# Attention loop: the outputs' turn moved from a head group's first step into its third

## The reference

```python
qkv = einsum('bsd,df->bsf', x, Wqkv) + bqkv        # 32 query heads, 8 key and value heads of 8
k = repeat(k, 4, axis=2); v = repeat(v, 4, axis=2)
scores = einsum('bqhd,bkhd->bhqk', q, k) / sqrt(8)
attn = softmax(scores, axis=-1)
out = einsum('bhqk,bkhd->bqhd', attn, v).reshape(b, s, 256)
return einsum('bsd,de->bse', out, Wo) + bo
```

## Time and profile before

| what | us |
|---|---|
| median of 3 runs | 661.53 (659.85 to 665.92) |
| profiled execution, own time | 660.77 |
| its span in the trace | 659.0 |
| TensorE busy in the span | 614.3 (93%) |
| VectorE busy | 395.3 (60%) |
| ScalarE busy | 327.2 (50%) |
| GpSimd busy | 251.4 (38%) |
| maxima, 256 of 682 ns | 156.6 busy |
| exponentials, 256 of 603 ns | 136.5 busy |

### The profile page before, as it was taken

One profiled execution on the slowest core, in us unless ns is written; L12 is line 12 of the kernel. 1 busy time (PEld: TensorE's weight loads), 2 busy tenths in 40 slices (PEclk: granted clock), 3 DMA queues, 4 the chain that ended last, 5 costly groups with the idle time before them and its releaser, 6 DMA issues.

```text
span 659.0 us, 11841 instructions
## 1 busy us (share of the span) xinstructions
PE 614.3 (93%) x4298; PEld 405.0 (61%) x4298; DVE 395.3 (60%) x916; ACT 327.2 (50%) x654; POOL 251.4 (38%) x331
## 2 busy tenths in 40 slices
PE   3999999999999989999979999999999999999990
PEld 2887887888788775566666444444444445556650
DVE  5426705732670578433366989898989955743326
ACT  4523423432342234244315589898989875423322
POOL 5870561282065063413333033635253520431331
PEclk9999999999999999999979999999999999999995
DMA  6101200300189993222389994000000000031213
GB/s 223 33 1 33 97 0 6 124 1 1 33 262 298 109 261 124 87 67 81 108 254 346 304 178 4 1 2 1 2 2 1 1 2 1 17 98 53 85 57 127
DMA packets 69000, 57.40 MB, mean 87 GB/s; under 512 B 21520, under 2 KB 64400, under 8 KB 68944
## 3 DMA queue, kind: packets, MB, share of 16 engines
q1 hardware_dynamic: 66736, 50.60, 31.6%
q0 software_dynamic: 2208, 6.05, 2.5%
HBM read 30.78 MB, written 25.85 MB: 86 GB/s over the span
## 4 chain that ended last, share of the span: by engine, by line
PE 79%; DVE 9%; DMA 4%; ACT 3%; POOL 2%; issue 2%; another core or an unknown queue 1%; SPq 0%; ACTq 0%; POOLq 0%; DVEq 0%
PE psum L1670 10%; PE psum L306 9%; PE psum L308 9%; PE psum L307 9%; PE psum L1303 8%; PE psum L1642 8%; PE psum L1630 5%; PE psum L1332 4%; PE psum L1655 4%; DVE stat L655 2%; PE psum L1227 2%; PE psum L1600 2%; DVE mx L1782 1%; PE psum L1213 1%; PE psum L1220 1%
## 5 line engine op out<-in xcount | busy, mean ns | idle before, releaser
L1782 DVE TENSOR_REDUCE mx<-psum 128x1 f32<-128x512 f32 x256 | 156.6, 682 | 17.9 <-PE psum L1642 17.9
L1528 ACT ACTIVATE pr<-psum 128x512 f32<-128x512 f32 x256 | 136.5, 603 | 25.6 <-PE psum L1655 25.5
L1655 PE MATMUL psum<-qT,kT 32*128 32x512 f32 x256 | 77.5, 494 | 1.1 <-ACT pr L1528 1.1
L1670 PE MATMUL psum<-pr,vals 128*32 128x256 f32 x1024 | 77.6, 389 | 0.0
L1642 PE MATMUL psum<-kT,qT 32*128 32x512 f32 x256 | 64.4, 493 | 0.9 <-ACT qT L1495 0.7
L613 POOL DMA_INDIRECT routed_y<-yr,xg x30 | 28.7, 957 | 83.0 <-DVE yr L865 82.4
L1303 PE MATMUL psum<-w_gu,xgT 128*128 x120 | 56.4, 592 | 0.0
L1642 PEld LDWEIGHTS psum<-kT,qT 32*128 32x128 f32 x256 | 24.2, 181 | 43.7 <-DVE mx L1782 21.8
L856 DVE SCALAR_TENSOR_TENSOR h<-psum,xg,sg 128x256 f32<-128x256 f32 x30 | 14.5, 484 | 49.8 <-ACT sg L1058 49.8
L576 POOL TENSOR_TENSOR ksum_t<-k_hi 128x1024 f32<-128x1024 f32 x8 | 19.2, 2401 | 64.6 <-DVE k_lo L803 64.4
L1580 POOL CAST mp<-mx 128x16 bf16<-128x16 f32 x16 | 3.1, 197 | 105.8 <-DVE mx L1782 105.8
(11 more groups left out here) (218 smaller groups left out, 1419.0 us busy)
## 6 DMA issues: line engine op xcount, KB each, us to landing
sorted_x<-zeros SPq DMA_DIRECT2D x2, 9088.0 KB, 39.9
w_gu<-in_L_ffn_gate_w SPq DMA_DIRECT2D x16, 256.0 KB, 6.7
w_gu<-in_L_ffn_up_w SPq DMA_DIRECT2D x16, 256.0 KB, 6.5
w_d<-in_L_ffn_down_w SPq DMA_DIRECT2D x16, 256.0 KB, 6.4
xg<-sorted_x SPq DMA_DIRECT2D x30, 129.0 KB, 2.1
wk_f<-in_L_attn_Wk SPq DMA_DIRECT2D x4, 512.0 KB, 5.2
wq_f<-in_L_attn_Wq SPq DMA_DIRECT2D x4, 512.0 KB, 5.9
wv_f<-in_L_attn_Wv SPq DMA_DIRECT2D x4, 512.0 KB, 4.0
```

Of the source, the lines that this page charges most:

```text
L1528: nc.scalar.activation(pr[d % 3][:, j], s2_bank(d, j), ACT.Exp, scale=SCALE).then_inc(exp_ready, 1)
L1655: mm(s2_bank(d, j), kT[n // GH][rows, kc * P:(kc + 1) * P], qT2[n % 2][rows, :], start=True, stop=True).then_inc(s2_made, 1)
L1670: last = mm(ps[AV_BANK][j * VW:(j + 1) * VW, cols], vals[:, n // NKV * TB + kc, n % NKV // GH * GH + j, :], pr[d % 3][:, j, cols], start=( ...
L1782: v.tensor_reduce(mx[n % 2][:, t, j:j + 1], s1_bank(c, j), AX.X, ALU.max, negate=True).then_inc(max_read, 1)
```

## The change

The outputs' turn of group n leaves step 4n + 12 (a first step) for step 4n + 14 (a third step). On TensorE it stands ahead of the second half of the first scores instead of behind it. On VectorE its copy stands between the second and the third maximum of the step instead of behind all four. Outputs 13 to 15, in steps 64, 68 and 72, stay where they were. ScalarE's code is unchanged.

```diff
             if c % TB == 0:
-                what = [("q1", c // TB + 1), ("o", (c - 12) // TB)]
+                what = [("q1", c // TB + 1)] + ([("o", (c - 12) // TB)] if c >= STEPS else [])
...
             else:
-                what = []
+                what = [("o", (c - 14) // TB)] if c < STEPS else []
...
             if c_ < STEPS:
-                FOR_DVE += [("s1", c_ * GH + j) for j in range(GH)]
+                FOR_DVE += [("s1", c_ * GH + j) for j in range(2)]
                 FOR_DVE += [x_ for x_ in new if x_[0] == "o"]
+                FOR_DVE += [("s1", c_ * GH + j) for j in range(2, GH)]
...
                 for what in turns_at(c):
-                    if what[0] != "o":
+                    if what[0] != "o" or c < STEPS:
                         turn(what)
                 if c < STEPS:
                     scores1(c, 1)
                 for what in turns_at(c):
-                    if what[0] == "o":
+                    if what[0] == "o" and c >= STEPS:
                         if what[1] == NG - 1:
                             keep_warm(2, SPARE)
                         turn(what)
...
             for c in range(END):
-                n = (c - 12) // TB if c % TB == 0 and c >= 12 else -1
+                now = [n for kind, n in turns_at(c) if kind == "o"]
                 if c < STEPS:
-                    for j in range(GH):
-                        maximum(c, j)
+                    maximum(c, 0)
+                    maximum(c, 1)
+                    for n in now:
+                        outputs(n)
+                    maximum(c, 2)
+                    maximum(c, 3)
                 if QKV_AT <= c < QKV_AT + TB:
                     take(TB + c - QKV_AT)
-                if 0 <= n < NG:
-                    outputs(n)
+                if c >= STEPS:
+                    for n in now:
+                        outputs(n)
```

## The result

The changed kernel is slower by 0.75%: a ratio of 1.0075 to the kernel before, 95% interval 1.0057 to 1.0092, which on 660.3 us is 5.0 us. Its median is 665.75 us against 660.3 for 20 executions of each. The forecast was 666.5 from 661.53, +5.0, with a range of 663.2 to 669.6. Two of the 20 executions of the changed kernel took 1694 and 3168 us and are left out of the ratio (without them the median is 665.63).

The account below looks back on a forecast made before the run. The prediction took the loop to be a ring of TensorE, VectorE and ScalarE; third steps +4.4, first steps -0.1, +1.0 and -0.4, tail +0.2, fourth steps -0.1 gave +5.0, so 666.5 us, range 663.2 to 669.6.

Parts of the forecast that it names:

- ring of three banks: First step: the last second score waits for the second exponential to free a ScalarE bank; 3.37 us instead of 3.50.
- Rival A: First step not held by ScalarE: one slot of 0.43 us less per group, 5.6 us faster, 655.9 us; chance 0.07.
- The third step: Where the outputs' turn goes: 2.63 us, +0.34 rather than the turn's 0.59; 4.4 us over 13 groups.
- the old wait: Third step, second half: the last second score waits for an exponential to free a bank; takes in 0.25 of the turn.
- The carry: ScalarE's lateness from the third step passes through the fourth; ScalarE starts the first step 0.22 to 0.25 us later.
- the alternative 0.53: Second score to exponential takes 0.53 us, not 0.60: carry about 0.1, sum 3.5 to 4.0, 665.3 us.
- Rival B: No carry, ScalarE makes up 0.2 us in the fourth step: 663.9 us; chance 0.10.
- Rival C: VectorE's ring binds and holds the third step's fourth first score for 0.23 us: 3.0 more, 669.5 us; chance 0.11.
- The last touched group: Its first step, without q1: end set by ScalarE instead of VectorE, 3.08 us instead of 3.47, -0.4.
- the earliest first step: The one touched first step without lateness carried in from a group before: -0.1 us.
- the 11 with carry: First steps that ScalarE starts late: 3.59 us instead of 3.50, 11 x 0.09 = 1.0 us.
- tail of +0.2: Behind the last touched group: the tail starts with ScalarE late, +0.2 us.

Follow-up runs that it names:

- e1: Against the kernel before: outputs' turn stays in the first step but stands between the step's halves on TensorE and VectorE; ratio 0.9977.
- e2: Against the kernel before: the 13 outputs' turns left out, VectorE copies a constant from SBUF instead; ratio 0.9968.
- e3: The changed kernel with ScalarE's copy to oT moved behind the exponentials of heads 2 and 3 in touched first steps; ratio to the kernel before 1.0039.
- e6: The changed kernel with one PSUM bank moved from VectorE's ring (three left) to ScalarE's (four); ratio to the kernel before 1.0071.
- e5: The changed kernel with the outputs' turn in the third step but behind the second half of the first scores; ratio to the kernel before 1.0168.
- e4: The changed kernel with only VectorE's copy put back behind the four maxima of the third step; ratio to the kernel before 1.0229.
- e7: On top of e1: second scores issued ahead of first scores in each step's first half, from the 7th step on; ratio to the kernel before 0.9968.

## Why the prediction was right

- **No slot is won in the first step.** Forecast: 3.37 without carry, held by the ring of three banks, although TensorE alone would need 2.49. e1 and e2 gave 3.37 each, e3 and e6 moved only what ScalarE does or owns and shortened the step. Rival A is excluded, and with it the rule that pairing by itself is a gain: it was, by 0.13.
- **The third step pays 0.34 of the turn's 0.59.** Measured 2.64 against 2.30. The rest lies in the old wait; e5 shows that this holds behind the first scores too, where a slot is paid on top.
- **The carry.** Forecast 0.22 to 0.25 from the third exponential of the third step, over the bank wait of the fourth, into ScalarE's start of the first. Measured: exponential 0.59 behind its score (0.60 taken; the alternative 0.53 is out), bank wait 0.22, oT copy at 0.49 instead of 0.28, first step 3.55 to 3.59. e4 removes the carry and finds 3.37. Rival B is excluded.
- **VectorE hides its copy.** No first score of the changed kernel waits for it. Rival C did not happen; e4 shows how near it was: two maxima later, and the copy adds 1.05 to the fourth step, 0.87 to the group.
- **The last touched group.** Its first step was 3.06 after 3.48, -0.4 as said, and for the reason given: it starts at 525.00, and its last second score is released by ScalarE 1.64 into it (1.65 forecast).

```profile
526.64 0.49 PE L1656 MATMUL psum<-qT,kT 32*128 32x512 f32 x1 [0.20 <-ACT pr L1529]
```

- **The sum.** +5.0 forecast, +5.0 by the ratio (3.8 to 6.1). Term by term, in the profiled loop: third steps +4.4 (4.4 forecast), the earliest first step -0.1 (-0.1), the 11 with carry +0.7 (1.0, so this term was 0.3 too large), the last -0.4 (-0.4), fourth steps 0.0 (-0.1): +4.6 against 4.8. The tail of +0.2 cannot be read from the changed kernel's trace, since a dip of the clock lies in it; in e3, which has the same tail and no dip there, it was 0.17 longer than before. That the total came out at 5.0 to the digit is luck. It could not have told the forecast from my alternative of 3.5 to 4.0; the 0.59 of the exponential does. And 666.5 was too high by 0.75, less than the 1.2 by which the median of three that it started from lay above that of 20.

The two parts of the change have opposite signs: "between the halves" alone gained 0.12 per group in the first step, "into the third step" alone lost 0.77, and together they lose 0.4. They do not simply add up: the place between the halves is worth 0.12 per group in the old step and 0.37 in the new one (11.66 to 11.29), because there no bank of ScalarE's holds up the slot it saves.

## What to carry to other kernels

In a ring of engines, an operation that looks like load on the busiest engine may stand in a hole that another engine's bank order has made; before moving it, ask when the next item behind it could start without it. Where it goes to, count how much of it falls into a wait already there, and then follow the delay once around the ring, past the steps whose length does not change: here most of e7's gain in three steps (0.16 of 0.2) was lost in the first step, and in the change a delay made in the third step cost 0.2 in the first, more than the 0.13 won there by taking the turn out, while the step between them kept its length. An engine at 100% busy proved nothing; step lengths over repeated groups resolved hundredths of a microsecond where the total time could hardly tell 0.3%.

## What the runs showed that I had not expected

In the profiled executions of e4, e5, e6 and e7 TensorE's granted clock fell for a short stretch early in the loop, near 380 us, where the other five, the kernel before and the changed kernel among them, kept it. In e5 (columns as in the earlier trace rows):

```profile
376.00:378.50 2.50, 1.95 (x13) 0.97 (x12) 2.40 (x5) 1.91 (x4) 0.00 (x0) 1.00 1.10 329
378.50:382.30 3.80, 3.80 (x29) 1.57 (x28) 3.02 (x5) 2.82 (x6) 2.84 (x10) 0.55 1.12 275
382.30:386.00 3.70, 3.70 (x44) 1.67 (x40) 2.88 (x5) 2.87 (x6) 0.17 (x1) 1.00 1.12 282
```

The step there took 4.89 us against 3.72 in the changed kernel: 1.2 us for one dip to the lower of the two levels (1.2 of 2.4 GHz), ahead of which TensorE had been idle for 0.55 of 2.5 us. That idle time is not what sets these kernels apart: the kernel before was idle for 0.53 of 2.7 us at the same place (376.0 to 378.7 us) and kept 1.00. In e4 and e5 the code up to that step is the same as in kernels that had no dip there, so it is not an effect of their edits that the traces could show.

The changed kernel had its dip elsewhere, behind the loop. The kernel before (first row) had one low stretch in mid-kernel, ahead of the loop, twice as long as the changed kernel's (second row), and none behind it:

```profile
334.30:341.10 6.80, 5.45 (x25) 5.45 (x26) 5.86 (x21) 0.00 (x0) 1.29 (x2) 0.50 0.95 288
...
333.70:337.10 3.40, 2.88 (x13) 2.88 (x14) 3.29 (x14) 0.00 (x0) 0.00 (x0) 0.50 0.98 294
538.50:541.90 3.40, 3.40 (x24) 1.22 (x21) 0.42 (x1) 0.95 (x3) 3.13 (x2) 0.50 0.02 5
```

Ahead of the loop the low stretch was 6.8 us long in the traces of before, e1, e2, e3 and e6, and 3.4 us in those of the changed kernel, e4, e5 and e7; each of the latter had a second one of 3.4 us later, and so had e6. What decides is open; one profiled execution of each kernel can't tell whether it goes with the kernel. For a comparison of two traces it means: take step lengths from stretches with a clock of 1.00, and before a difference of one or two microseconds in the span is put down to an edit, look where the clock was low in each.
